# Attention on one core: TensorE turns the probabilities of two units in a row before it issues their two scores

## The reference

```python
x = x + attention(layernorm(x), ctx, mask)      # 16 heads of 32 channels, 2 key/value heads
# attention: Q, K rotated (rope); scores = Q K^T / sqrt(32), masked
#            attn = softmax(scores); out = attn V; out @ wo
x = x + ffn(layernorm(x))                       # 8 experts, the best 2 per token, and a shared one
```

## Time and profile before

| | us |
|---|---|
| median of 3 runs | 1408.04 (1407.82 to 1408.26) |
| the profiled execution, whole | 1408.64 |
| its span, first to last instruction | 1406.8 |

### The profile page before, as it was taken

The page is one execution under the profiler, slowest core; times in us unless marked ns, Lnnn a source line. Parts: engine busy times, 40 slices in busy tenths (PEclk is TensorE's granted clock), DMA queues, the critical chain, the costliest instruction groups (busy, mean ns, idle before and its releaser), DMA issues.

```text
span 1406.8 us, 28203 instructions
## 1 busy us (share of the span) xinstructions
PE 1339.5 (95%) x8061; PEld 1025.5 (73%) x8061; DVE 959.3 (68%) x2665; ACT 836.6 (59%) x1951; POOL 581.3 (41%) x724
## 2 busy tenths in 40 slices
PE   6898999999999999999898999999999999999997
PEld 4675776767767677676565777777778888888885
DVE  6888989888897888988776666666653433334332
ACT  2788979889798897988983222222213333334332
POOL 3443433434344253342254333333343555555553
PEclk9799999999999999999999999999999999999999
DMA  6545464564644646545366232222257879786552
GB/s 205 149 134 152 130 193 144 144 200 136 193 144 134 201 138 181 153 139 162 104 199 216 73 101 85 82 89 84 76 174 183 216 160 279 193 196 106 111 77 37
DMA packets 145780, 206.53 MB, mean 147 GB/s; under 512 B 35295, under 2 KB 72799, under 8 KB 145634
## 3 DMA queue, kind: packets, MB, share of 16 engines
q1 hardware_dynamic: 124274, 166.84, 38.7%
q0 software_dynamic: 17952, 33.64, 12.7%
q10 hardware_dynamic: 3408, 4.26, 0.9%
HBM read 105.42 MB, written 69.35 MB: 124 GB/s over the span
## 4 chain that ended last, share of the span: by engine, by line
PE 73%; ACT 11%; DVE 5%; issue 3%; DMA 3%; POOL 3%; SPq 2%; DVEq 0%; POOLq 0%; ACTq 0%
PE psum L1505 13%; PE psum L1507 13%; PE psum L1506 13%; PE psum L695 7%; PE psum L810 6%; ACT a_probs L593 6%; PE psum L789 6%; ACT a_probsT L599 3%; PE psum L740 3%; PE psum L742 3%; PE psum L741 3%; PE psum L1572 1%; PE psum L1601 1%; PE psum L710 1%; DVE a_probs L957 1%
## 5 line engine op out<-in xcount | busy, mean ns | idle before, releaser
L593 ACT ACTIVATE a_probs<-a_probs,a_low 128x512 f32<-128x512 f32 x512 | 366.4, 716 | 82.3 <-DVE a_low L957 82.0
L957 DVE CUSTOM_DVE_ANT_0 a_probs<-psum,a_bias 128x512 f32<-128x512 f32 x512 | 343.7, 685 | 70.3 <-PE psum L789 66.9
L695 PEld LDWEIGHTS psum<-a_ident_r,a_probs_bits 128*128 128x128 f32 x2048 | 225.8, 142 | 88.1 <-issue 28.2
L695 PE MATMUL psum<-a_ident_r,a_probs_bits 128*128 128x128 f32 x2048 | 247.1, 245 | 14.9 <-ACT a_probsT L599 8.6
L789 PE MATMUL psum<-a_kT,a_q_stack 128*128 128x512 f32 x512 | 245.7, 481 | 13.4 <-DVE a_low L957 7.7
L599 ACT ACTIVATE a_probsT<-psum 128x512 f32<-128x512 f32 x328 | 189.9, 580 | 5.4 <-PE psum L695 4.7
L1374 POOL DMA_INDIRECT out<-b_y,b_pairs_sb x71 | 112.6, 1586 | 149.8 <-DMA out<-b_y,b_pairs_sb 79.8
L963 DVE COPY a_probsT<-psum 128x512 f32<-128x512 f32 x184 | 126.0, 685 | 2.8 <-PE psum L695 1.7
L1807 DVE SCALAR_TENSOR_TENSOR b_v_hidden<-b_v_hidden,psum 128x256 f32<-128x256 f32 x71 | 29.9, 421 | 134.3 <-ACT b_v_hidden L1470 89.5
L810 PE MATMUL psum<-a_probsT,a_v 128*32 128x512 f32 x1024 | 117.7, 600 | 0.0
L1505 PE MATMUL psum<-b_w,b_vT_hi 128*128 x284 | 116.6, 410 | 0.0
(11 more groups left out here) (221 smaller groups left out, 2973.1 us busy)
## 6 DMA issues: line engine op xcount, KB each, us to landing
b_w<-w_halves SPq DMA_DIRECT2D x16, 1536.0 KB
a_q_stack<-a_qT_hi SPq DMA_DIRECT2D x254, 64.0 KB, 2.0
a_q_stack<-a_qT_lo SPq DMA_DIRECT2D x253, 64.0 KB, 2.0
w_halves<-a_w_hi SPq DMA_DIRECT2D x96, 128.0 KB, 2.0
w_halves<-a_w_lo SPq DMA_DIRECT2D x96, 128.0 KB, 1.9
a_xT_in<-in_x_turned SPq DMA_DIRECT2D x32, 256.0 KB, 2.9
a_ctx_in<-in_ctx SPq DMA_DIRECT2D x32, 256.0 KB, 3.0
a_x_in<-in_x SPq DMA_DIRECT2D x32, 256.0 KB, 3.2
```

The source lines that it names most:

```text
L593: nc.scalar.activation(probs[:, h % 2, t], probs[:, h % 2, t], ACT.Exp, bias=low[:, h % H, t:t + 1], scale=-1.0, accum_out=total[:, h // G ...
L695: last = nc.tensor.transpose(out[:, P * i:P * (i + 1)].bitcast(F32R), src(i), ident_r[:])
L957: nc.vector.tensor_tensor_reduce(probs[:, h % 2, t], psum[:, t % 2], bias[:, t], 1.0, HUGE, ALU.add, ALU.min, low[:, h % H, t:t + 1]).then ...
```

## The change

The units are taken in pairs (u, u + 1), u even. PE turns u and u + 1 (eight transposes in a row); then it does the turns (kT, qT, inverse) that the table lists for u; then the score of u + 6 and the rest of u's other work; then the score of u + 7 and u + 1's other work, its own turns last. `line` is rebuilt in this order. Nothing else moves: the tables, the loops of the other engines and all DMAs are as before.

```diff
     RINGED = ("kv", "kT", "qT", "inverse", "spread")
+    TURNED = ("kT", "qT", "inverse")
+
+    def beside_pair(u):
+
+        first, second = PE_AT.get(u, ()), PE_AT.get(u + 1, ())
+        later = [p for p in second if p[0] in TURNED]
+        return [p for p in first if p[0] in TURNED], [p for p in first if p[0] not in TURNED], [p for p in second if p[0] not in TURNED] + later
+
     line = []
-    for u in range(H * TT):
-        line.append(("probs", u))
-        line += [(kind, i) for kind, i in PE_AT.get(u, ()) if kind in RINGED]
+    for u in range(0, H * TT, 2):
+        turns, first, second = beside_pair(u)
+        line += [("probs", u), ("probs", u + 1)]
+        line += [(kind, i) for kind, i in turns + first + second if kind in RINGED]
...
-        def beside(part, b, par, u):
-            for kind, i in stages(part, PE_AT, u):
+        def beside(part, b, par, u, places):
+            for kind, i in places:
+                if not there(part, kind, i):
+                    continue
...
-            for u in range(H * TT):
-                turn_probs(part, b, u // TT, u % TT)
-                if u + AHEAD < H * TT or part != "last":
-                    scores(b, par, (u + AHEAD) // TT, u % TT ^ 2)
-                beside(part, b, par, u)
+            for u in range(0, H * TT, 2):
+                turns, first, second = beside_pair(u)
+                for w in (u, u + 1):
+                    turn_probs(part, b, w // TT, w % TT)
+                beside(part, b, par, u, turns)
+                for w, others in ((u, first), (u + 1, second)):
+                    if w + AHEAD < H * TT or part != "last":
+                        scores(b, par, (w + AHEAD) // TT, w % TT ^ 2)
+                    beside(part, b, par, w, others)
```

## The result

| | before | after |
|---|---|---|
| median of four runs, us | 1407.93 (1407.63 to 1408.26) | 1459.59 (1458.49 to 1465.38) |
| profiled execution, whole, us | 1408.64 | 1465.38 |
| its span, us | 1406.8 | 1463.3 |

The ratio is 1.0378, with a 95% interval of 1.0356 to 1.0401: **slower by 51.7 us**. I predicted slower by 9.8 (1417.8, range 1401.5 to 1426.0): the sign was right, the size was wrong by a factor of five, and the result lies outside the range. The profiled execution is the slowest of the four, 56.7 above the profiled one of before.

A forecast was written before the change was run, and what follows sets the result against it. PE looked like the bound at 95% busy, but took turns with ACT within a batch. Terms summed to 1.35 us per middle batch, 8.1 for six, plus 0.78 and 0.94: +9.8, so 1417.8 us, range 1401.5 to 1426.

The forecast's parts named there:

- Everything else I cost at nothing: Moved kT and qT of other units, and unit 49's kT now behind AV: no cost.
- (c): Units 16 and 17: two scores instead of one stand between the query turn and AV, +0.22 us per middle batch.
- (e): Units 22 to 29: unit 25's bank wait partly freed, inverse turn's bank later; +0.2 us, from -0.15 to +0.5.
- PE's saving: About 0.025 us per pair where PE paces, some 11 of 32 pairs: 0.27 us per batch.
- the bounds that I chose: A score behind a score on PE takes between 0.23 and 0.30 us; 0.23 was taken.
- (a): Unit 1: both scores stand behind the turn that waits for ACT's evacuation, so AV starts later, +0.22 us.
- (b): Unit 2: score behind unit 3's turns, delaying the exp that starts ACT's gapless 13.4 us, +0.35 us.
- (f): Unit 52: four more turns ahead of the score delay the exp opening ACT's second gapless stretch, +0.3 us.
- (d): Units 20 and 21: unit 21's four turns go ahead of the query projection that DVE waits for, +0.33 us.
- Gain: Rival, chance 0.23: late first scores are absorbed, only PE's saving stands, up to 6.4 us, about 1402.
- no change: Rival, chance 0.14: ACT catches up at AV of unit 33, PE's saving offsets unit 52's delay, about 1408.
- Slower by the clock: Rival, chance 0.08: longer waits at units 1 and 16 to 17 make the clock fall each batch, about 1432.

The follow-up runs named there:

- e9: Kernel before, with turns paired only at the 19 even units whose own other work takes no bank of the ring: 1417.90 us, ratio 1.0066.
- e10: Kernel before, with turns paired only at the other 13 even units, where a bank is emptied one evacuation later: 1440.86 us, ratio 1.0231.
- e12: Changed kernel, with units 26 and 27 evacuated by DVE and 25 by ACT, to shorten the wait at unit 29: 1450.72 us, ratio 1.0294.
- e13: Changed kernel, with two POOL subtractions held until DVE has made the inverse row sums: 1457.22 us, ratio 1.0367.
- e14: e12 with two POOL subtractions held until DVE has made the inverse row sums: 1446.49 us, ratio 1.0274.
- e16: Control: kernel before, with two POOL subtractions held until DVE has made the inverse row sums: 1409.69 us, ratio 1.0023.
- e2: Kernel before, units left single, with only the even units' own turns (kT, qT, inverse) moved ahead of that unit's score: 1408.93 us, ratio 1.0010.
- e8: Kernel before, with pairs only at units 36 to 49 and the score ahead of the turn at unit 2: 1410.90 us, ratio 1.0010.
- e7: Kernel before, with the pair of turns at units 2 and 52 alone: 1413.46 us, ratio 1.0028.
- e1: Changed kernel, pair kept, but the even unit's other turns (kT, qT, inverse) put back behind that unit's score: 1442.78 us, ratio 1.0246.
- e5: Changed kernel, with only the list of units evacuated by DVE altered so that late banks are emptied sooner: 1440.77 us, ratio 1.0226.
- e15: e5 with two POOL subtractions held until DVE has made the inverse row sums: 1440.50 us, ratio 1.0240.

## Why the prediction was wrong in size

**The step that failed** is one sentence: "Everything else I cost at nothing: the moved kT and qT of other units". I had seen that the list of banks shifts, and used it in (c) and (e), but not gone through the rest of it: of its 84 entries 44 wait for another release than before, and 32 of these lie outside the units of (c) and (e). What the runs showed in place of that nothing is waits for banks that are emptied one evacuation later, 33.6 us of PE's time over the six middle batches instead of 3.3, with scores queued behind them. So the sign was right in the main for another reason than mine: of the 51.7 us, the late scores that I had priced make some 10 (e9). A middle batch of the change takes 95.2 to 95.8 us, some 7.6 more than before. By the runs that is:

| cause | us per middle batch | from |
|---|---|---|
| late scores, less PE's saving | 1.06 | e9 |
| banks one evacuation later, with the scores behind them | 3.7 | e10 (3.6 in its two batches without a POOL collision or a fall) |
| one more fall of the clock | 1.4 to 1.5 | e12's rows, e13's batches |
| DVE behind POOL | 0.4 to 0.55, perhaps up to 1.1 | e13, e14, control e16; a little of it in the row of e10 |

Together 6.6 to 6.8 with POOL at 0.4 to 0.55. The remaining 0.8 to 1.0 was not isolated; POOL at its most would be 0.6 of it. The one move that is in neither e9 nor e10, unit 49's kT behind AV, is not it: from unit 48 to unit 50 exp falls back by nothing. On the whole time, e9 and e10 give 10 + 33 = 43 of 51.7 us, and e12, whose clock doesn't fall at unit 29, gives 41. No version that I ran is faster than the kernel before; e2 and e8 can't be told from it.

**PE's price held.** Eight turns take 0.63 us (I took 0.65), a score with no turns ahead of it 0.23, the end of the bounds that I chose. The Trainium skill, TensorE: Matmul & The Clock Gate, section "Step-by-step: what each phase is for", has the load pulled ahead of a running matmul. The trace agrees: the load (PEld) for the score at 340.51 takes 0.19 us while the product before it runs.

```profile
340.28 0.39 PE L751 MATMUL psum<-a_wq_hi,a_xT_lo 128*128 128x512 f32 x1
340.28 0.19 PEld L798 LDWEIGHTS psum<-a_kT,a_q_stack 128*128 128x128 f32 x1
```

**(a) and (b) held, (f) where it stood alone; (d) did not.** At unit 2 ACT's idle time before exp is 0.94 us, where I had named 0.95:

```profile
333.54 0.72 ACT L602 ACTIVATE a_probs<-a_probs,a_low 128x512 f32<-128x512 f32 x1 [0.94 <-DVE a_low L972]
```

e7 gives 0.35 for (b) and 0.35 for (f), where I had 0.35 and 0.3. In e9, AV at unit 1 (a group is 32 matmuls in the trace, not 64) starts 0.98 us behind its turn, where I had named 0.96 (in the change it is 1.26), and exp behind unit 2 is 0.58 us late; (a) + (b) were 0.57. All the terms of e9's pairs, (a) + (b) + (d) + (f) - 0.27, sum to 0.93, and it measured 1.06. That the sum fits is partly luck: e9's exps fall back by 0.3 at unit 16 and again at unit 34, which no term of its pairs names, and by 0.1 at units 20 and 21, where (d) has 0.33; what unit 52 takes there, 0.2, unit 51 had just given back. In the change itself exp does not fall back at units 20 and 21, and DVE's wait for the query, which I had put at 1.5 us, is 7.3 us, 6 times, as before.

**(c) and (e) were too small.** In the change exp falls back by 1.6 us at unit 17, of which 0.96 is the collision with POOL (e13); the other 0.7 is still three times the 0.22. In units 22 to 25 it falls back by 0.3 to 0.6 instead of 0.2, read against a kernel whose own batches scatter by 0.9 there: unit 25's wait of 0.55 us, which (e) wanted to free, stands in only three of the six batches. Then in units 28 to 33, where I had costed the key turn and what follows at nothing, it falls back by another 3.4 (0.6 of it given back by unit 39): the key turn of 28, the clock behind it, and the second collision. At units 8 to 11, also costed at nothing, the inverse turn and the spread take 1.0.

**The rivals.** Gain and no change did not happen, in spite of PE's 95%: the change made PE wait, and a busy share cannot show a wait that is not yet there. "Slower by the clock" did happen as a mechanism, a little under the price that I gave as the most (half of 3.4 us each; 1.4 to 1.5), but not at the place I named: the wait behind which the clock falls is at unit 29, and it is one of the new bank waits.

## What to carry to other kernels

In a ring of buffers that is filled in program order, moving one user ahead makes every entry that it passes wait for a release one place later; before costing the move at nothing, write both lists side by side and name, for each entry, who must have emptied its buffer. On an engine that works in order the price of such a wait is not the wait alone, but all that is queued behind it. What is won by joining work on one engine is small where that engine spends much of its time feeding others in turn.

## What the runs showed of the hardware

The granted clock fell to 0.51 for 3.4 us behind PE's wait at unit 29. Where that wait was 1.67 to 1.69 us in all six middle batches, it fell in six of them (the change), in four (e13) and in two (e10); where it was 1.38 to 1.39 (e1), in one; where it was 1.20 to 1.24 (e5, e12, e14, e15), in none. One fall cost 1.37 to 1.50 us. A DVE subtraction of 128x16 elements took 1.15 us instead of 0.18 when a POOL subtraction of 128x512 had begun just ahead of it.
